# Two buffers for the experts' transposed input, and an output row sum made by an accumulating transfer

## What is computed

```python
h = layernorm(x) * (1 + ca) + sa
x = x + ga * mamba(h)                    # in_proj, conv, selective scan over 16 states, gate, out_proj; + h
h = layernorm(x) * (1 + cb) + sb
g = sigmoid(h @ gate_w.T)                # router over 16 experts, the best 4 kept and normalised to `combine`
act = silu(h @ e_win) * (h @ e_vin) * combine     # 16 routed experts; a shared one of twice the width, unweighted
x = x + gb * (routed + shared)           # act @ e_wout, summed over the experts
```

## Time and profile before

| | |
|---|---|
| median of 3 runs | 2781.83 us (2780.56 to 2785.82) |
| the profiled execution's own time | 2781.71 us |
| its span, first to last instruction | 2779.9 us |
| mean granted TensorE clock over the span | 0.921 of full speed |
| first scan, and the end of the last | 79.0 and 2660.2 us after the start |

### The profile page before, as it was taken

How to read it: one execution, slowest core, us unless ns; L and a number is a source line. 1 busy time by engine, 2 the same in 40 slices (tenths; PEclk the granted TensorE clock), 3 DMA queues, 4 the chain that set the end, 5 groups by cost and what they waited for, 6 DMA issues and landing times.

```text
span 2779.9 us, 51800 instructions
## 1 busy us (share of the span) xinstructions
PE 2395.2 (86%) x16084; PEld 1915.6 (69%) x16084; DVE 2360.0 (85%) x3751; ACT 1977.6 (71%) x3777; POOL 2280.8 (82%) x2254
## 2 busy tenths in 40 slices
PE   4557989989798898979989798988989898898989
PEld 1334777768677686867768586776868677686867
DVE  4888989898898989889898898889888898988853
ACT  4786877778677777867677786777778777786631
POOL 2777898979889798988979899797988979798942
PEclk7658999989899998999999999999989999899999
DMA  2575666757567575665757565674756667476731
GB/s 84 159 161 111 142 152 142 166 121 161 121 146 169 126 165 129 146 144 139 160 121 175 135 140 132 155 169 111 165 128 145 142 151 160 114 161 147 159 85 56
DMA packets 136128, 388.85 MB, mean 140 GB/s; under 512 B 20232, under 2 KB 22920, under 8 KB 135600
## 3 DMA queue, kind: packets, MB, share of 16 engines
q0 software_dynamic: 55296, 201.35, 39.1%
q1 hardware_dynamic: 80560, 184.20, 20.7%
HBM read 166.29 MB, written 17.87 MB: 66 GB/s over the span
## 4 chain that ended last, share of the span: by engine, by line
PE 32%; POOL 26%; issue 18%; DVE 10%; ACT 8%; DMA 3%; POOLq 0%; DVEq 0%; ACTq 0%; SPq 0%
PE bank_ps L1469 13%; POOL db_sb L711 12%; PE moe_ps L1487 7%; PE rows_ps L1405 6%; DVE states L1194 4%; POOL act L754 4%; POOL y_sb L723 3%; POOL y_sb L732 2%; PE bank_ps L1353 2%; POOL du_sb L698 2%; ACT da_ps L955 2%; PE bank_ps L1365 2%; DMA y_sb<-c_rows 2%; DVE c_rows L1236 1%; ACT c_rows L928 1%
## 5 line engine op out<-in xcount | busy, mean ns | idle before, releaser
L711 POOL TENSOR_TENSOR db_sb<-du_sb,b_sb 128x512 f32<-128x512 f32 x1024 | 1498.5, 1696 | 33.4 <-DVE states L1194 33.3
L955 ACT ACTIVATE da_ps<-delta,a_sb 128x512 f32<-128x512 f32 x1024 | 704.9, 692 | 136.1 <-DVE states L1194 132.4
L1405 PE MATMUL rows_ps<-ident,states 128*128 128x128 f32 x4096 | 627.8, 291 | 142.2 <-DVE states L1194 102.4
L1469 PE MATMUL bank_ps<-h2T_high,ein_w_high 128*128 128x256 f16 x2304 | 646.6, 281 | 49.8 <-DVE delta L1168 20.7
L754 POOL TENSOR_TENSOR act<-act,w_sb 128x256 f32<-128x256 f32 x512 | 506.3, 1142 | 206.8 <-DVE act L1291 184.0
L1405 PEld LDWEIGHTS rows_ps<-ident,states 128*128 128x128 f32 x4096 | 509.4, 150 | 236.9 <-DVE states L1194 113.3
L1194 DVE TENSOR_TENSOR_SCAN states<-da_ps,carry,db_sb 128x512 f32<-128x512 f32 x512 | 648.1, 1276 | 5.2 <-ACT da_ps L955 3.1
L1469 PE MATMUL bank_ps<-h2T_high,ein_w_low 128*128 128x256 f16 x2304 | 645.5, 280 | 0.0
L1469 PE MATMUL bank_ps<-h2T_low,ein_w_high 128*128 128x256 f16 x2304 | 644.4, 280 | 0.0
L1194 DVE TENSOR_TENSOR_SCAN states<-da_ps,db_sb 128x512 f32<-128x512 f32 x512 | 616.6, 1216 | 13.3 <-ACT da_ps L955 12.5
L1487 PE MATMUL moe_ps<-eout_sb,act 128*128 128x256 f32 x2304 | 577.9, 384 | 10.9 <-POOL act L754 10.8
(11 more groups left out here) (169 smaller groups left out, 2685.6 us busy)
## 6 DMA issues: line engine op xcount, KB each, us to landing
y_sb<-c_rows POOLq DMA_DIRECT2D x384, 512.0 KB, 5.3
b_sb<-b_dram SPq DMA_DIRECT2D x128, 512.0 KB, 5.2
w_sb<-w_dram SPq DMA_DIRECT2D x256, 256.0 KB, 3.6
th_p<-x_dram SPq DMA_DIRECT2D x16, 512.0 KB, 5.3
r_dram<-conv SPq DMA_DIRECT2D x16, 512.0 KB, 5.0
x<-r_dram SPq DMA_DIRECT2D x16, 512.0 KB, 3.7
out_dram<-x SPq DMA_DIRECT2D x32, 256.0 KB, 5.5
mod_p<-mod_dram SPq DMA_DIRECT2D x7, 384.0 KB, 4.4
```

The lines of the kernel that those rows point to most:

```text
L711: pool.tensor_tensor(db_sb[:, n % NDB, :], du_sb[:, slots[t][0][0], b, :], b_sb[:, k % NBPAIR, s % BPAIR, :], ALU.mult).then_inc(sem["scal ...
L955: ac.activation(da_ps[n % NDA][:, :], delta[:, slots[t][0][0], b, :], ACT.Exp, scale=a_sb[:, b, s:s + 1]).then_inc(sem["exp_done"], 1)
L1405: last = pe.transpose(rows_ps[j % 2][:, b * P:b * P + P], states[:, step % 2 * NB + b, j * P:j * P + P], ident[:, :])
L1469: last = pe.matmul(bank(key)[:, a * HALF:a * HALF + HALF], ein_w16[w][:, k, e // 2, at:at + HID], h2T[h][:, k, q * HALF:q * HALF + HALF], ...
```

## The change

- `h2T` gets two buffers, one for each parity of the chunk. The room comes from `wT` and `weigh`, which move into `zg`. `h2_high` now waits for the experts of the chunk before the last one.
- `x1` is stored whole to the output by a new step, `x1_store` (SP), once its four parts are summed.
- `out_gate` writes its product to on-chip memory: half 0 into the first half of `x1`, half 1 into the chunk's own `h2T` high half, read as fp32. `out_add` and `out_store` go. A new step `out_join` (POOL) adds that buffer to the stored rows in DRAM with an accumulating DMA.
- The next `r_load` waits for the store and for the join of half 0 alone. The row of the gate is loaded by a step of its own, `mod_g_load`.
- All constants of the planner are others: `SHIFT`, `PLACE`, `FIRST`, `LAST`, `START` and the scalars. So the order changes everywhere.

```diff
+    out.append((5.5, ("x1_store", t)))
...
-            out += [(at + 1.75 + TICK, ("out_gate", t, u // NALL)), (at + 1.76 + TICK, ("out_add", t, u // NALL)),
-                    (at + 1.77 + TICK, ("out_store", t, u // NALL))]
+            out += [(at + 1.75 + TICK, ("out_gate", t, u // NALL)), (at + 1.76 + TICK, ("out_join", t, u // NALL))]
...
-TICK, ROUTED, UNITS_END = 1.4006, 15.946, 63.7625
+TICK, ROUTED, UNITS_END = 1.6007, 16.0741, 63.9904
...
-SLOT = 70.0828
+SLOT = 70.2916
...
+    out += [(SLOT * t + 20.0, t, 0, ("mod_g_load", t)) for t in load_mod_m]
...
-        h2T = [sb(f"h2T_{n}", [P, NK, CH], F16) for n in ("high", "low")]
+        h2T = [sb(f"h2T_{n}", [P, 2, NK, CH], F16) for n in ("high", "low")]
...
-        wT = sb("wT", [NE, CH])[:, :]
+        wT = zg[0:NE, 1, :]
...
-        weigh = sb("weigh", [P, NJ, NE])
+        weigh = zg[:, 0, 0:NJ * NE].rearrange("p (j e) -> p j e", j=NJ)
...
+            def gated(t, q):
+
+                if q == 0:
+                    return x1[:, 0:2, :]
+                return h2T[0][:, slots[t][2][0], :, :].rearrange("p k n -> p (k n)").bitcast(F32).rearrange("p (j n) -> p j n", j=2)
...
-                            sp.wait_ge(sem["y_out"], nM(t) * 32)
+                            sp.wait_ge(sem["y_out0"], 16 * nM(t))
+                            sp.wait_ge(sem["x1_out"], 16 * nM(t))
...
+                    def x1_store(t):
+
+                        for j in range(NJ):
+                            sp.wait_ge(*bank_read(("op", t, j)))
+                        sp.dma_start(out[bass.ds(slots[t][2][1], 1)].rearrange("o p j n -> (o p) j n"), x1[:, :, :]).then_inc(sem["x1_out"], 16)
...
+                    def out_join(t, q):
+
+                        pool.wait_ge(sem["out_gated"], 2 * nM(t) + q + 1)
+                        pool.wait_ge(sem["x1_out"], 16 * (nM(t) + 1))
+                        pool.dma_start(out[bass.ds(slots[t][2][1], 1), :, 2 * q:2 * q + 2, :].rearrange("o p j n -> (o p) j n"), gated(t, q),
+                                       accum_op=ALU.add).then_inc(sem[f"y_out{q}"], 16)
...
-                            ac.wait_ge(*bank_full(("expert_in", last, UNITS - 1)))
-                            ac.wait_ge(*bank_full(("expert_in", last, UNITS - 2)))
-                        ac.activation(h2T[0][:, k, :], bank(("h2_t", t, k)), ACT.Copy).then_inc(sem["h2_high_done"], 1)
+                            if nM(t) > 1:
+                                for u in range(UNITS - 2, UNITS):
+                                    ac.wait_ge(*bank_full(("expert_in", last_mix(last), u)))
+                                ac.wait_ge(sem["y_out1"], 16 * (nM(t) - 1))
+                        ac.activation(h2T[0][:, slots[t][2][0], k, :], bank(("h2_t", t, k)), ACT.Copy).then_inc(sem["h2_high_done"], 1)
...
-                        v.tensor_tensor(moe_ps[:, :, :], moe_ps[:, :, :], mod_m[:, 1:2, :].broadcast_to([P, 2, DM]), ALU.mult).then_inc(sem["out_gated"], 1)
-
-                    def out_add(t, q):
-                        v.wait_ge(sem["out_gated"], 2 * nM(t) + q + 1)
-                        place = x1[:, 2 * q:2 * q + 2, :]
-                        v.tensor_tensor(place, place, moe_ps[:, :, :], ALU.add).then_inc(sem["out_added"], 1)
+                        v.wait_ge(sem["mod_in_g"], 16 * rows_in(load_mod_m, t))
+                        v.wait_ge(sem["x1_out"], 16 * (nM(t) + 1))
+                        v.wait_ge(sem["x1_normed"], NJ * (nM(t) + 1))
+                        v.tensor_tensor(gated(t, q), moe_ps[:, :, :], mod_m[:, 1:2, :].broadcast_to([P, 2, DM]), ALU.mult).then_inc(sem["out_gated"], 1)
```

More of the change, by code:

```diff
@@ L245 @@
-LAST = {"e_act": -0.013, "e_mul": 0.055, "e_tanh": 7.665, "e_weigh": 9.991, "expert_in": 1.282, "expert_out": 1.728, "h2_high": -2.579,
-        "h2_low": -1.883, "h2_scale": -3.705, "h2_t": -3.18, "logit": -5.063, "logit_exp": -1.443, "op": -1.223, "op_gate": 0.698,
-        "out_add": 0.395, "out_gate": 1.049, "out_store": 2.058, "r_load": 1.578, "router": -1.085, "w_evac": 7.703, "w_load": 4.992,
-        "w_store": 0.751, "w_t": 1.21, "x1": 0.98, "x1_norm": -2.829, "x1_rstd": -3.726, "x1_stat": 0.952, "y_evac": 0.855,
-        "y_gate": -1.648, "y_t": -1.423, "z": -3.218, "z_gate": -0.524, "z_tanh": -0.384}
@@ new lines @@
+LAST = {"e_act": 0.289, "e_mul": 0.423, "e_tanh": -0.433, "e_weigh": -2.123, "expert_in": -0.009, "expert_out": 0.773, "h2_high": 1.164,
+        "h2_low": 0.419, "h2_scale": 0.205, "h2_t": -2.733, "logit": -0.34, "logit_exp": -0.58, "op": 1.392, "op_gate": 0.002,
+        "out_add": 0.012, "out_gate": -0.18, "out_join": -3.238, "r_load": -17.439, "router": 0.196, "w_evac": 1.983, "w_load": 10.695,
+        "w_store": -0.513, "w_t": 1.119, "x1": 0.004, "x1_norm": -4.893, "x1_rstd": 3.963, "x1_stat": 2.849, "x1_store": -3.094,
+        "y_evac": -2.93, "y_gate": 4.985, "y_t": 1.386, "z": -2.795, "z_gate": -3.817, "z_tanh": -3.195}
@@ L255, in place @@
+START = {"a_made": 0.885, "constants": 0.343, "ct_silu": -19.772, "ct_tanh": -7.189, "first_loads": -2.134, "fold": 1.188,
+         "in_high": -16.361, "in_low": -17.039, "mod0": -16.514, "mod0_gate": -3.544, "mod0_rows": -2.728, "mod_rows": 1.506,
+         "mod_store": 11.99, "mods": -15.428, "norm_lift": -10.097, "out_scale": -6.894}
 def place(what):
@@ L637, in _ @@
                     sp.wait_ge(sem["b_stored"], 16 * nP(len(slots)))
-                    sp.wait_ge(sem["y_out"], 32 * nM(len(slots)))
+                    sp.wait_ge(sem["x1_out"], 16 * nM(len(slots)))
+                    for q in range(2):
+                        sp.wait_ge(sem[f"y_out{q}"], 16 * nM(len(slots)))
                 @block.gpsimd
@@ L1447, in logit @@
                             for n, (k, h, w) in enumerate(SPLIT):
-                                last = pe.matmul(bank(key)[:, j * NE:j * NE + NE], h2T[h][:, k, j * P:j * P + P], gate_w16[w][:, k, :],
+                                last = pe.matmul(bank(key)[:, j * NE:j * NE + NE], h2T[h][:, slots[t][2][0], k, j * P:j * P + P], gate_w16[w][:, k, :],
                                                  start=(n == 0), stop=(n == len(SPLIT) - 1))
@@ L1469, in expert_in @@
                                 last = pe.matmul(bank(key)[:, a * HALF:a * HALF + HALF], ein_w16[w][:, k, e // 2, at:at + HID],
-                                                 h2T[h][:, k, q * HALF:q * HALF + HALF], start=(n == 0), stop=(n == len(SPLIT) - 1))
+                                                 h2T[h][:, slots[t][2][0], k, q * HALF:q * HALF + HALF], start=(n == 0), stop=(n == len(SPLIT) - 1))
                         last.then_inc(bank_full(key)[0], 1)
@@ L1484, in expert_out @@
                         if first:
-                            pe.wait_ge(sem["out_added"], 2 * nM(t) + q)
+                            pe.wait_ge(sem["out_gated"], 2 * nM(t) + q)
                         for n in range(2):
```

90 lines of the change are left out of this document (42 added, 48 removed), and 144 rows, old and new, of the table PLACE.

## The result

The changed kernel takes 2803.9 us (median of 4 runs, 2799.9 to 2805.1), the kernel before 2782.5: ratio 1.0074, 95% interval 1.0059 to 1.0089. It is slower by 0.74%. The forecast of 2773 was wrong in sign; the time lies in the range, next to the figure of the rival "the joins decide", 2802, for reasons that are only partly that rival's.

The account below looks back on a forecast made before the run. No engine far ahead: PE, DVE and POOL bound in turn, POOL in about 60 us per slot. Boundaries 9.8 us less, start +1.8, drain -1.7, last DMA +0.5: together -9.2 against 2781.7, giving 2773; range 2748 to 2808.

Parts of the forecast that it names:

- the joins decide: Rival, slower: POOL is full where both joins are issued; 32 x 0.61 = +19.5 us, giving 2802; chance 0.35.
- (a): Before `h2T` is overwritten: the wait on the experts has 39 us of slack, so the second buffer is worth 0.
- (b, c): DVE loses 32 `out_add`, 20.8 us, counted 0 or 0.65 per slot; SP loses two waits on `out_added`, 0.
- (c): On SP, the next `b_load` and `r_load` lose two waits on `out_added`; no boundary wait ends on them: 0.
- (d): `out_gate` on DVE keeps its 0.70 us row; half 1's 1.17 us wait should shrink; counted 0, at most 1.1 per slot.
- (f): Two more DMA issues per chunk on POOL: 0.61 us per join, 0.90 at the far end; all 32 on the path, 19.5.
- DVE's extra scan: Rival, no change: one more `scan` before the last `x1_stat` makes POOL wait 1.1 us instead of 0.46; 2782; chance 0.20.
- (e): DMA traffic: 16 stores of 512 KB replace 32 of 256 KB, plus 32 joins of 256 KB, 2% more traffic; 0.
- Start +1.8: At the start, `out_scale` ahead of the first `x_rstd` on POOL costs 5.9 us, partly regained: net +1.8 us.
- a sign I had named: At the start: a first scan later than 81 us would show the forecast wrong.
- Drain -1.7: At the end, PE's two `z` and two `expert_out` now precede the last scan step's `rows`: 1.7 of 4.3 us gained.
- last DMA +0.5: At the end, a join issued where `out_add` began lands 2.0 to 5.4 us later, 2778.7 to 2782.1; taken +0.5 us.

Follow-up runs that it names:

- the kernel with one join: Changed kernel with one accumulating transfer of 512 KB a chunk in place of two of 256 KB, `r_load` at 8 us: 2765.6 us, ratio 0.9930.
- a bare issue: Kernel before plus two plain 16-byte-per-partition transfers a chunk issued by GpSimd, nobody waiting for them: 2789.7 us, ratio 1.0017.
- kernel with the last join moved: Against the kernel with one 512 KB join a chunk, the last chunk but one's join is due 9 units later: 2774.2 us, ratio 0.9966.

## Why the prediction was wrong

- **The second buffer is worth 0** (a): right, 0.9994.
- **`out_add` gone and SP's waits gone, 0 each** (b, c): in the sum they and the new order were to give, without any join, 2772.5 - 19.5 = 2753 us. Without joins the changed kernel takes 2766, and 2751 with `r_load` clear of the `c_add`s. So that part was near in sum, with `r_load` where the forecast left it, but by luck in its pieces: there the 14 slots are 32 us shorter (2257.4 against 2289.5), where the forecast's own terms give 26 (14 x (1.22 + 0.61)), the start is 6.6 us shorter where 1.8 longer was forecast, and the stretch behind the last scan is 8.9 longer where 1.7 shorter was.
- **"The next `b_load` and `r_load` no longer stand behind them; no wait of the boundary ends on these loads, so 0"** (c): this step failed too. I asked who waits for `r_load`, not whom it meets when it starts some 17 us earlier. It costs 15 us without the joins (2766.4 - 2751.5), 4 with them under the new order, 18 under the old.
- **(d), the wait before `out_gate` "should shrink"**: it grew, for half 1, from 26.3 us in all to 65.0. With `r_load` clear of the `c_add`s, and without joins, it is 44.2. I had counted 0 for it.
- **The joins** (f), 0.61 us each, paid for by moved work: this is the step that decides the miss. The measured time is 31 us above the forecast. Taking the joins away takes 37.5 us off; putting `r_load` right and keeping both joins takes off 4.2. The queue moves on after 0.57 to 0.62 us, as read, and POOL was busy 0.96 for each; the time grew by 37.5 / 32 = 1.17, by 0.9 for the first issue of a chunk and 1.7 to 1.9 for the second. The sum had let moved work pay for each join at the boundary (0.61 - 1.22) and in POOL's full stretch (0); the runs show no such payment. The price was read off POOL's queue alone. What a late POOL does to TensorE, which at the boundary idled 5.5 of 23.3 us, had no term; its waits for the `y_gate`s are 10 to 14 us longer with the second issue, and the rest of the price stays open.
- **What bounds the kernel**: the text ahead of the prediction, and the prediction, put the DMA issues of POOL on top of its 82%. They are in it: the 2254 instructions of the earlier trace rows hold the 384 `c_add`s. Over the whole span POOL is less full than was argued.
- **No wait for `out_gated`**: right but for one wait of 3.5 and one of 2.4 us; the 9.0 us in front of the half 1 joins have no named cause.
- **DVE's extra scan**: `x1_rstd` waits for DVE now (30.2 us, 16 times, 12.4 of it at the end), but the kernel with one join has 26.2 of it and is the fastest of those that leave nothing out. Not the cause.
- **Stores and traffic 0** (e): the joins' bytes are some 5 us, at the edge of what the runs resolve. The early store was not tried apart.
- **Start +1.8**: the first scan came 4.5 later, a sign I had named; the other kernels of the new order, with the same start, have it at 80.8 to 83.1 us. But the second chunk's first scan followed 8.2 us sooner, so the net was -3.7.
- **Drain -1.7, last DMA +0.5**: the stretch behind the last scan grew by 12.9. I priced the new order of PE there and not the join in POOL's queue in front of the last `y_gate`s, nor the chain `logit`, `w_store`, `w_load`, on whose load POOL waits 24.1 us (before 18.5). The last join landed 4.4 us after its issue, inside the bounds. (The prediction's other figure for it, 2.6 us, would have ended the sum 1.1 us earlier than my 0.5, not 0.1.)

The table of the Trainium skill's page "DMA: Bandwidth & Descriptors", section "SWDGE vs HWDGE vs iDMA", says that a transfer that accumulates is issued by GpSimd and a plain one by SP. The prediction took that as speaking against this change, and the runs agree in this kernel: a free store on SP became an issue on GpSimd at 0.9 to 1.9 us. In the kernel before, under the old order, a bare issue is 0.13 us.

The rival's 2802 met the time, 2803.9, by 19.5 us added to a base of 2782; the runs show 37.5 added to a base of 2766. That it came so near was luck.

## What to carry to other kernels

Don't price an added instruction by its queue time alone; ask what the delayed engine feeds, and measure. Here the same issue cost 0.13 us in one order of the steps and 1.9 in another. When a wait is removed, look at what starts earlier and at whose transfers it will meet; a load that nobody waits for moved the time by 42 us between three places. If a transfer must be issued by a loaded engine, issue few and large ones: one join of 512 KB for a chunk in place of two of 256 KB turned +0.7% into -0.7%, and 27 of the 38 us come back when that one join is split in two.

## What the hardware showed that I had not expected

- An issue on GpSimd takes the same time whatever it carries: for the join of half 1 877 ns with 256 KB and 876 with 8 KB, for that of half 0 1168 and 1158; and 0.57 us to the next instruction with 256 and with 512 KB.
- `r_load`'s 512 KB land in 6.2 us (median) when they start among the accumulating transfers, and in 3.4 when they start at 8 us or so (kernel with the last join moved); the accumulating one beside it takes up to 9.8 in place of 5.8.
- TensorE's time at the lower clock grew from 71 to 108 us in 14 slots with 16 more issues of 0.6 us on another engine. But 17 us more of it in the same 14 slots went with 5.5 us more of TensorE's busy time and only 2.2 us of length.
